# Attention of four images: the products of the second head pair before the values, keys repeated by DMA, and token sums copied by ScalarE

## The reference, cut to what matters

```python
q = (h1 @ wq).reshape(b, l, H, DK)
k = (h1 @ wk).reshape(b, l, H, DK)
v = (h1 @ wv).reshape(b, l, H, DV)
qw = jnp.einsum('bihd,hdn->bihn', q, w_pos)
qr = jnp.einsum('bihn,ijn->bhij', qw, basis)
bias = (qr + uk + vr) * scale
scores = jnp.einsum('bihd,bjhd->bhij', q, k) * scale + bias
attn = jax.nn.softmax(scores, axis=-1)
out = jnp.einsum('bhij,bjhd->bihd', attn, v)
out = out.reshape(b, l, H * DV) @ wo + bo
```

## Time and profile before

| | us |
|---|---|
| median of 3 runs | 986.55 (982.59 to 987.46) |
| the profiled execution | 989.25 |
| its span | 987.5 |

### The profile page before, as it was taken

The page is one execution under the profiler, slowest core; times in us unless marked ns, Lnnn a source line. Parts: engine busy times, 40 slices in busy tenths (PEclk is TensorE's granted clock), DMA queues, the critical chain, the costliest instruction groups (busy, mean ns, idle before and its releaser), DMA issues. The chain is left out here.

```text
span 987.5 us, 19877 instructions
## 1 busy us (share of the span) xinstructions
PE 882.2 (89%) x6415; PEld 783.3 (79%) x6415; DVE 703.0 (71%) x1654; ACT 650.2 (66%) x1222; POOL 138.7 (14%) x205
## 2 busy tenths in 40 slices
PE   5999999999996699879988998898699996799996
PEld 5999999999986577667766776766597885699995
DVE  6889869869834786589748875886665235687775
ACT  5767757648724797689769885986643331776862
...
GB/s 275 23 64 62 39 64 37 21 138 150 146 105 62 217 288 212 55 237 296 173 73 252 289 143 114 225 273 94 107 1 1 32 82 17 132 151 98 72 1 65
DMA packets 85259, 120.63 MB, mean 122 GB/s; under 512 B 12655, under 2 KB 44988, under 8 KB 85116
## 3 DMA queue, kind: packets, MB, share of 16 engines
...
## 5 line engine op out<-in xcount | busy, mean ns | idle before, releaser
L481 PE MATMUL psum<-w,feat 128*128 128x192 f32 x912 | 160.1, 330 | 12.2 <-ACT feat L398 9.1
L481 PEld LDWEIGHTS psum<-w,feat 128*128 128x128 f32 x912 | 149.0, 192 | 13.0 <-issue 10.5
L732 POOL TENSOR_SCALAR a_scores<-a_scores,a_inv 112x514 f32<-112x514 f32 (+1 forms) x160 | 111.9, 700 | 257.2 <-DVE a_inv L1108 257.2
L1093 DVE CUSTOM_DVE_ANT_0 a_scores<-psum,a_bias 112x514 f32<-112x514 f32 (+1 forms) x160 | 109.9, 687 | 42.4 <-PE psum L801 33.8
L962 ACT ACTIVATE a_scores<-a_scores,a_least 112x514 f32<-112x514 f32 (+1 forms) x160 | 117.0, 731 | 6.4 <-DVE a_least L1093 6.0
L813 PE MATMUL psum<-ident,a_scores 112*112 112x112 f32 (+1 forms) x800 | 101.8, 258 | 14.4 <-ACT a_probsT L957 7.6
L499 PE MATMUL psum<-w_parts,parts 128*128 128x384 f32 x368 | 113.7, 374 | 0.8 <-DVE parts L253 0.8
L398 ACT ACTIVATE feat<-turn 128x1024 f32<-128x1024 f32 (+1 forms) x60 | 58.4, 974 | 80.7 <-PE psum L501 42.4
L813 PEld LDWEIGHTS psum<-ident,a_scores 112*112 112x112 f32 (+1 forms) x800 | 75.6, 134 | 39.0 <-POOL a_scores L732 22.8
L801 PE MATMUL psum<-a_kh,a_q 128*112 128x258 f32 (+1 forms) x320 | 105.6, 351 | 0.0
L501 PE MATMUL psum<-w_parts,parts 128*128 128x192 f32 x384 | 96.6, 252 | 0.0
...
## 6 DMA issues: line engine op xcount, KB each, us to landing
shear<-a_pos SPq DMA_DIRECT2D x128, 224.4 KB, 3.9
a_bias<-shear SPq DMA_DIRECT2D x128, 224.4 KB, 3.9
...
shear<-a_pos SPq DMA_DIRECT2D x32, 130.3 KB
a_bias<-shear SPq DMA_DIRECT2D x32, 130.3 KB
```

What stands on the lines that cost most here:

```text
L481: mm = pe.matmul(sums[m][:, 0:D], feat[:, r, j, 0, 128 * m:128 * m + 128], w[:, k, :], start=begins, stop=ends)
L732: pool.tensor_scalar(row, row, inv[0:TILES[g % NT][1], g % TT:g % TT + 1], 1.0, ALU.mult, ALU.mult).then_inc(weighed, 1)
L1093: dve.tensor_tensor_reduce(halves(scores[0:r, g % TT, 0:PADL]), psum2(score_pair(g), r), halves(bias[0:r, g % MR, :]), -1.0 / 8, BIG, ALU. ...
```

## The change

- `EARLY` is 6: q1 and k1 stand before the values in `PRODS`. In the tail k0 goes to pair 0, q1 to pair 2 (around `flip(39)`, which now comes before the values) and k1 to pair 0 (behind `values(1, 0)`). Seven products are left in the front, in pairs 3, 1, 0, 3, 1, 0, 3.
- Keys are repeated by SP's DMAs, `kh` and `kl` of one pair of heads each: those of pairs 0 and 1 at the end of the image before, those of pairs 2 and 3 at SP's steps 14 and 16. The load of x moves from step 8 to step 18. The copies on ScalarE and VectorE go.
- Positions 0 to 9 alternate between banks 4 and 5; 0 and 1 stand ahead of all products of the front.
- The output projection uses bank 5 and the first bank of pair 1.
- ScalarE makes the copies of the token sums of the first three images, behind the sine of group 1; those of the last stay on VectorE.

The diff, cut to its core:

```diff
             def take_sums(i):
-                dve.wait_ge(base_set, i + 1)
                 for m in range(4):
-                    dve.wait_ge(sums_done, i * 4 + m + 1)
-                    dve.tensor_copy(tokens[:, m, :], sums[m][:, 0:D]).then_inc(stated, 1)
-                for m in range(4):
-                    dve.wait_ge(stated, i * 8 + m + 1)
+                    dve.wait_ge(sums_out, i * 4 + m + 1)
                     dve.tensor_tensor(tokens[:, m, :], tokens[:, m, :], sums[m][:, D:2 * D], ALU.add).then_inc(tokens_done, 1)
                 for m in range(4):
                     dve.wait_ge(tokens_done, i * 4 + m + 1)
                     dve.bn_stats(stats[:, m, :], tokens[:, m, :]).then_inc(stated, 1)
...
                 act.activation(feat[:, r, 0, 0:n, :], turn[:, r, 0:n, :], ACT.Sin, scale=TWO_PI).then_inc(sin_done, 1)
+                if not first and g == 1:
+                    copy_sums(b - 1)
...
+            def copy_sums(i):
+                act.wait_ge(base_set, i + 1)
+                for m in range(4):
+                    act.wait_ge(sums_done, i * 4 + m + 1)
+                    act.copy(tokens[:, m, :], sums[m][:, 0:D]).then_inc(sums_out, 1)
...
-    PRODS = [("p", 0), ("p", 1), ("q", 0), ("k", 0), ("v", (0, 1)), ("v", (2, 3)), ("v", (4,))] + [
-        (k, p) for p in range(1, H1 // 2) for k in "qk"]
-    EARLY = 4
+    PRODS = [("p", 0), ("p", 1), ("q", 0), ("k", 0), ("q", 1), ("k", 1), ("v", (0, 1)), ("v", (2, 3)), ("v", (4,)),
+             ("q", 2), ("k", 2), ("q", 3), ("k", 3)]
+    K0, Q1, K1 = 3, 4, 5
+    EARLY = 6
     EARLY_TILES = {NG - 10: 0, NG - 7: 1, NG - 4: 2}
-    LAST_EARLY = EARLY - 1
-    early_pair = lambda n, first: (3, 1, 0, 2)[n] if first else 2
-    late_pair = lambda n: (3, 1, 0, 3, 1, 0, 1, 2, 3)[n - EARLY]
+    early_pair = lambda n, first: ((3, 1, 0, 2, 3, 1) if first else (2, 2, 2, 0, 2, 0))[n]
+    late_pair = lambda n: (3, 1, 0, 3, 1, 0, 3)[n - EARLY]
+    K_PRODS = {p: n for n, (kind, p) in enumerate(PRODS) if kind == "k"}
     last_late = lambda n, pair: max([m for m in range(EARLY, n) if late_pair(m) == pair], default=None)
 
-    BEHIND = ((5, 0), (5, 1), (6, 0), (7, 0), (7, 1), (8, 0), (8, 1), (9, 0), (9, 1), (10, 0))
-    after_product = lambda n, w: [g for g, place in enumerate(BEHIND) if place == (n, w)]
+    BEHIND = {2: (6, 0), 3: (6, 1), 4: (7, 1), 5: (8, 0), 6: (9, 1), 7: (10, 0), 8: (10, 1), 9: (11, 0)}
+    after_product = lambda n, w: [g for g, place in BEHIND.items() if place == (n, w)]
+    POS_BANK, SUM_BANK = 4, 5
+    pos_bank = lambda g: SUM_BANK if g < AHEAD and g % 2 else POS_BANK
+    last_position = lambda g: max([e for e in range(g) if pos_bank(e) == pos_bank(g)], default=None)
...
+        PROJECT = (s.bank[SUM_BANK], pairs[1][0])
...
+            def repeat(i, p):
+
+                for x, ready, n_ready, repeated in ((kh, hi_done, i * NHI + first_parts(K_PRODS[p]) + 2, repeated_h),
+                                                    (kl, s.lo_done, i * H1 + 2 * p + 2, repeated_l)):
+                    sp.wait_ge(ready, n_ready)
+                    sp.dma_start(x[DK1:128, 2 * p:2 * p + 2, 0:PADL].bitcast(F32), x[0:DK1, 2 * p:2 * p + 2, 0:PADL].bitcast(F32)).then_inc(repeated, 16)
+
             def image(b, more):
                 for g in range(NG + LAG):
-                    if more and g == 8:
+                    if g in (14, 16):
+                        repeat(b, {14: 2, 16: 3}[g])
+                    if more and g == 18:
...
                     stack(b + 1, 0)
                     stack(b + 1, 1)
+                    repeat(b + 1, 0)
+                    repeat(b + 1, 1)
...
+            repeat(0, 0)
+            repeat(0, 1)
...
                 def position(g):
                     h, t = divmod(g, NT)
                     i0, r = TILES[t]
+                    if last_position(g) is not None:
+                        wait_position_out(last_position(g))
                     if g == 0:
                         pe.wait_ge(prod_free, b * NP + EARLY)
-                    else:
-                        wait_position_out(g)
-                    if g == AHEAD:
-                        pe.wait_ge(prod_free, b * NP + last_late(NP, 2) + 1)
-                    if g == 0:
                         pe.wait_ge(table_set, 1)
+                    if g == 1:
+                        pe.wait_ge(image_done, b * 2 + 1)
                     if h % G4 == 0 and t == 0:
                         pe.wait_ge(stacked[h // G4], 16 * 3 * G4 * (b + 1))
-                    pe.matmul(s.bank[POS_BANK][0:r, 0:POSW], qpos[:, h, i0:i0 + r], table[:, 0:POSW],
+                    pe.matmul(s.bank[pos_bank(g)][0:r, 0:POSW], qpos[:, h, i0:i0 + r], table[:, 0:POSW],
                               start=True, stop=True).then_inc(pos_done, 1)
...
                     if t == 0:
-                        pe.wait_ge(repeated_h, b * H1 + h + 1)
-                        pe.wait_ge(repeated_l, b * H1 + h + 1)
+                        pe.wait_ge(repeated_h, 16 * (b * (H1 // 2) + h // 2 + 1))
+                        pe.wait_ge(repeated_l, 16 * (b * (H1 // 2) + h // 2 + 1))
...
+                        else:
+                            wait_position_out(AHEAD - 1)
...
                 def project(w):
                     pe.wait_ge(values_out, b * 4 + 2 + w + 1)
+                    if more and w == 0:
+                        pe.wait_ge(prod_free, b * NP + NP + Q1 + 1)
                     for j in range(2):
                         i0 = 1 + 128 * (2 * w + j)
                         for hg in range(2):
-                            mm = pe.matmul(pairs[0][w][:, D * j:D * j + D], on[:, hg, i0:i0 + 128], wo[:, hg, :], start=hg == 0, stop=hg == 1)
+                            mm = pe.matmul(PROJECT[w][:, D * j:D * j + D], on[:, hg, i0:i0 + 128], wo[:, hg, :], start=hg == 0, stop=hg == 1)
                     mm.then_inc(wo_done, 1)
 
                 def late_product(n):
-                    if n == EARLY:
-                        pe.wait_ge(prod_free, EARLY)
-                    elif late_pair(n) == 2:
-                        wait_position_out(AHEAD)
-                    elif last_late(n, late_pair(n)) is None:
+                    if last_late(n, late_pair(n)) is not None:
+                        pe.wait_ge(prod_free, b * NP + last_late(n, late_pair(n)) + 1)
+                    elif late_pair(n) == 1:
                         pe.wait_ge(image_done, b * 2 + 2)
-                    else:
-                        pe.wait_ge(prod_free, b * NP + last_late(n, late_pair(n)) + 1)
...
                 def early_product(n, w):
 
-                    if w == 0 and n:
-                        pe.wait_ge(prod_free, b * NP + NP + n)
-                    elif w == 0:
+                    if n == 0 and w == 0:
                         pe.wait_ge(image_in, b * 16 + 16)
-                        wait_position_out(NG)
+                        wait_position_out(NG - 1)
+                        wait_position_out(NG - 2)
                     elif n == 0:
                         pe.wait_ge(values_out, b * 4 + 2)
+                    elif n == K0 and w == 0:
+                        pe.wait_ge(biased, b * NG + NG - 1)
+                    elif w == 0:
+                        pe.wait_ge(prod_free, b * NP + NP + (K0 if n == Q1 else K0 + 1 if n == K1 else n))
                     product(b + 1, n, early_pair(n, False), windows=(w,))
 
+                position(0)
+                position(1)
...
-                    early_product(LAST_EARLY, 0)
+                    early_product(K0, 0)
                 flip(NG - 3)
                 if more:
-                    early_product(LAST_EARLY, 1)
+                    early_product(K0, 1)
                 flip(NG - 2)
+                if more:
+                    early_product(Q1, 0)
+                flip(NG - 1)
+                if more:
+                    early_product(Q1, 1)
                 for jb in range(NT):
                     values(1, 0, jb, NG - 2)
-                flip(NG - 1)
+                if more:
+                    early_product(K1, 0)
+                    early_product(K1, 1)
                 project(0)
                 for jb in range(NT):
                     values(1, 1, jb, NG)
                 project(1)
...
+                if n >= Q1:
+                    pe.wait_ge(prod_free, n - Q1 + 1)
...
-            def repeat(i, n):
-
-                kind, p = PRODS[n]
-                if kind == "k":
-                    for e in range(2):
-                        h = 2 * p + e
-                        act.wait_ge(hi_done, i * NHI + first_parts(n) + e + 1)
-                        act.copy(kh[DK1:128, h, 0:PADL], kh[0:DK1, h, 0:PADL].bitcast(F32)).then_inc(repeated_h, 1)
...
+                position_out(0)
+                position_out(1)
...
-                    if g == 3:
-                        repeat(b, NP - 1)
...
                 put(NG - 3)
+                if more:
```

(23 more changed lines are left out.)

38 lines of the change are left out of this document (13 added, 25 removed).

## The result

The changed kernel takes 1025.09 us in the median (1022.41 to 1027.05), against 986.59 of the kernel before on the same chip: ratio 1.0414, interval [1.0371, 1.0457]. It is slower by 38.5 us, where I had forecast 978.6 and a range up to 989. The profiled execution took 1025.87 us, its span is 1024.0.

What follows compares the result with a forecast made beforehand. The prediction took four resources (TensorE, ScalarE, VectorE, DMA engines) to be at their limits in the attention loop, with gains in the seams. Its terms summed to -7.9 us, from 986.55 to 978.6 us, range 968 to 989.

Steps and rivals of the forecast that it cites:

- DMAs in the loop: Attention loop: key repeats and the load of x delay position stores and hold up copies, +6.8 us (0 to +13.8).
- Rival C: Attention loop: the DMA engines become its bound, +13.8 in place of +6.8, giving 985.6 us; chance 0.18.
- The front: Last projection to next image's first transposition: fewer products and copies, 18.5 us for 24.16, 3 x -5.7 = -17.1 us.
- The tail: End of each of three images: added products q1 and k1 lengthen it, +2.5 us each, +7.5 in all.
- Image 0: First image's front: four more DMAs ahead of the first store, offset by products in idle time, 0 us (-3 to +3).
- The end of image 3: Last image's tail: project(0) waits for ScalarE's copy after the reordered transposition 39, +1.0 us (0 to +2).
- Token sums: Three embedding seams: ScalarE's copies let the first sum start earlier, 3 x -0.7 = -2.1 us (0 to -3).
- The loop: Attention loop, tiles 3 and 4: k3's repeat leaves ScalarE and VectorE, -1.0 x 4 = -4.0 us (0 to -5).
- Rival D: Next image's first store, late behind the repeats, makes VectorE stand in the front three times: 997.6 us; chance 0.08.
- Rival E: Three attention seams: TensorE's clock falls to 0.50 as in image 0, giving about 1011 us; chance 0.05.

Runs made afterwards that it cites:

- e14: Changed kernel with the idle instructions of e10 ahead of TensorE's attention loop and the input load back at step 8: 1006.8 us, ratio 1.0212.
- e10: Changed kernel with 40 already met waits (20 instructions) ahead of TensorE's attention loop, shifting its code: 1016.7 us, one execution.
- e5: Kernel before with only the next image's input load moved from step 8 to step 18: 1001.3 us, ratio 1.0190.
- e15: Kernel before with only the keys' second copies moved to GpSimd, placed as in e9: 980.8 us, ratio 0.9978.
- e8: Changed kernel with the keys' second copies on GpSimd, TensorE's loop written out and the load at step 8: 984.1 us, ratio 1.0018.
- e9: e8 with GpSimd's copies of pairs 1 and 2 ahead of the first weighing and the last image's old tail order: 974.3 us, ratio 0.9914.
- e4: Kernel before with the keys' second copies by DMA and the input load at step 18 instead of 8: 1023.4 us, ratio 1.0362.
- e6: Kernel before with the keys' second copies by DMA and the input load left at step 8: 1005.6 us, ratio 1.0190.
- e3: Kernel before with only the change's token sums copied by ScalarE: 982.9 us, ratio 0.9982.
- e12: e6 with each repeat DMA moving only 64 of 514 columns, so part of the scores is left out: 984.4 us, ratio 1.0006.

## Why the prediction was wrong, by its own steps

The loss comes apart in steps that the runs share: before 985.07, with the new order, the token sums and repeats by DMA 1006.8 (e14), with the load at step 18 1016.7 (e10), with the loop in its bad place 1025.1. That is 21.7 + 10.0 + 8.4. Each step is good to a few us only: e10 is one execution, and executions of one kernel lie up to 15 us apart (e5, e15). By the parts of an image, in the two traces: fronts -0.3 in sum, loops +27.3, tails +12.6, image 0 up to its first transposition +2.7, and 5.4 us less behind the attention, where nothing was changed.

- **DMAs in the loop, +6.8 (0 to +13.8): the step that failed.** The bytes, the slack of 5.0 us for a store and the mechanism were right. Wrong was the 4.2 us: it is what a store takes in a loop without a burst, and I kept it inside the burst, where stores took 6.6 us (7.5 in e5). And I stopped at the standstill itself: each one idles TensorE, and then the clock is at 0.50 for some 7 to 14 us. By the stretches shown, TensorE stands idle for some 6 us from 459.8 to 479.8 and loses some 3 more by the clock (4 and 2.5 in e5), an estimate from busy time and granted clock. Measured in the kernel before, repeats 21 to 24 and the load's place 18 to 19; in the new order the load's place 10. My upper bound was below either of the first two. Rival C had the cause and a third of its size.
- **The move of the load to step 18 had no line of its own in the sum.** I counted it as one more burst. In e5 it costs some 19 us by itself, although it adds not a byte.
- **The front, 3 x -5.7: right where the code stayed in reach, a little too large.** The fronts are 19.1 to 20.4 there (I had 18.5), 3.8 to 4.8 less than before (e8, e9, e10, e14). The wait of score tile 0 for VectorE, which I named and gave no size, is 2.2 to 3.3 us there and in the changed kernel. But its 4.4 us for copies that leave the two engines is partly a loan: in e15 the same copies left, the fronts fell by 1.6 and the loops rose by 1.8, 2.2, 1.9 and 0.7. The work ahead of transposition 0 got shorter, the stream of positions through stores and loads did not. From position 0 to the issue of the last store it takes 65.3, 65.7 and 65.2 us in images 1 to 3 before and 65.8, 65.9 and 64.4 in e15. I had summed seam and loop as if each ended on its own.
- **The tail, +2.5: nearly right.** 15.1 us in each of the first three images, +3.3, in every version with the new order. Against the fronts' 4.5 that leaves 1.2 us a seam, where I had 3.2; and 1.5 of the 4.5 come with the copies that leave (e4, e15), so the order alone wins nothing at the seam. What it gains stands in the loops, some 8 us in sum (e14 against e6, e9 against e15).
- **Image 0, 0 (-3 to +3): inside its bounds, at the edge.** The first transposition came 2.7 us later (344.26 for 341.60): the first store left 3.4 us later. In e9, without the four repeats ahead of it, it came at 338.05.
- **The end of image 3, +1.0 (0 to +2): too small.** 13.2 us against 10.4, up to 15.8 in e8 and e10. The wait was as I had it, the lowered clock behind it was not in the sum.
- **Token sums, -2.1:** -1.2 by the seams' waits, too small to measure in the whole (e3).
- **The loop, -4.0:** not found. In e12 and e15 the copies of k3 are gone from both engines, and no loop is shorter.
- **Rival D** (store 0 of the next image behind the repeats) did not happen: in images 1 to 3 the first store leaves 1.0 to 1.1 us after position 0. **Rival E** named a clock of 0.50 in the fronts, and there it was, for part of each front. In images 1 and 2 it stands behind gaps that I had nowhere, those at the branch; the place of the code, a cause outside the diff's semantics, had no line in my list. And my argument against it, no gap above 1.3 us, did not hold either: the change's own wait at score tile 0 makes one of 2.2 to 2.3 us in all three fronts, with 3.4 us at 0.50 behind it in image 3, and of 3.09 us with 10 us at 0.50 in e9's image 1.

What stays open: which places of a loop are bad, and why. Counted from where the kernel before has it, a start 40 instructions further on is bad with 1559 and with 1567 instructions a pass; good are 0 with either length, 60 with 1559 and 108 with 1567.
